# Retention's chunk loop: two output banks in turn, the outer product behind the next scores, and the state's masking, scaling and sum on GpSimd

## The reference, cut to what matters

```python
def _L3_attn_ref(x, Wq, Wk, Wv, gn_weight, gn_bias, Wout):   # 16 heads of 8
    Q = jnp.einsum('bld,hde->bhle', x, Wq)
    K = jnp.einsum('bld,hde->bhle', x, Wk)
    V = jnp.einsum('bld,hde->bhle', x, Wv)
    Dm = _decay_mask(Lq)                      # gamma_h ** (l - m) for m <= l, else 0
    scores = jnp.einsum('bhle,bhme->bhlm', Q, K) * Dm[None] / math.sqrt(HEAD_DIM)
    out = jnp.einsum('bhlm,bhme->bhle', scores, V)
    ...                                       # statistics over each head's whole length
    return combined @ Wout
```

## Time and profile before

| | us |
|---|---|
| median of 3 runs (2124.52 to 2133.64) | 2124.52 |
| the profiled execution: its own time | 2124.77 |
| the profiled execution: its span | 2123.0 |
| PE busy over the span | 1987.1 |
| DVE busy over the span | 1468.1 |
| ACT busy over the span | 1012.4 |
| POOL busy over the span | 260.6 |
| the chunk loop, first scores to last output (1923.67 to 1976.47) | 52.8 |

### The profile page before, as it was taken

How to read it: one execution, slowest core, us unless ns; L and a number is a source line. 1 busy time by engine, 2 the same in 40 slices (tenths; PEclk the granted TensorE clock), 3 DMA queues, 4 the chain that set the end, 5 groups by cost and what they waited for, 6 DMA issues and landing times.

```text
span 2123.0 us, 38784 instructions
## 1 busy us (share of the span) xinstructions
PE 1987.1 (94%) x13148; PEld 1242.4 (59%) x13148; DVE 1468.1 (69%) x4162; ACT 1012.4 (48%) x1898; POOL 260.6 (12%) x408
## 2 busy tenths in 40 slices
PE   7999999998999899999999998999997899998898
PEld 3523333333678556666666665778674677774576
DVE  6679999994566556666666666466658545877786
ACT  4347767776334355555555553345433333342233
POOL 2252212111027200000000000073000000000000
PEclk9989999999999999999999999999999999999999
DMA  6210000000027400000000000256100000000000
GB/s 238 32 63 26 26 23 28 23 23 24 16 74 220 123 1 1 1 0 0 0 0 0 0 1 1 75 164 206 51 1 0 1 1 1 1 1 2 1 1 21
DMA packets 62912, 78.07 MB, mean 37 GB/s; under 512 B 18954, under 2 KB 36638, under 8 KB 62017
## 3 DMA queue, kind: packets, MB, share of 16 engines
q1 hardware_dynamic: 57536, 67.18, 10.1%
q0 software_dynamic: 4672, 8.99, 1.7%
q10 hardware_dynamic: 576, 0.26, 0.1%
HBM read 64.14 MB, written 10.88 MB: 35 GB/s over the span
## 4 chain that ended last, share of the span: by engine, by line
PE 83%; DVE 7%; ACT 5%; issue 3%; DMA 1%; SPq 1%; ACTq 0%; POOL 0%; DVEq 0%; POOLq 0%
PE ps L455 13%; PE ps L434 12%; PE ps L1033 7%; PE ps L1067 6%; PE ps L2644 6%; PE ps L2607 6%; PE ps L2628 5%; PE ps L1050 4%; PE ps L835 3%; PE ps L846 3%; PE ps L2081 2%; PE ps L1017 2%; PE ps L1079 2%; ACT arena L1170 1%; PE ps L1039 1%
## 5 line engine op out<-in xcount | busy, mean ns | idle before, releaser
L455 PEld LDWEIGHTS ps<-l_w,arena 128*128 128x128 f32 x2560 | 335.4, 192 | 161.2 <-issue 144.1
L2894 DVE TENSOR_REDUCE arena<-ps 128x1 f32<-128x512 f32 x512 | 325.9, 684 | 40.9 <-PE ps L2607 40.9
L455 PE MATMUL ps<-l_w,arena 128*128 128x128 f32 x2560 | 339.3, 276 | 6.0 <-ACT arena L506 5.0
L434 PE MATMUL ps<-xnT,l_w 128*128 128x512 f32 x640 | 330.5, 599 | 3.0 <-ACT xnT L265 3.0
L2799 ACT ACTIVATE arena<-ps 128x1024 f32<-128x1024 f32 x256 | 252.6, 1022 | 102.1 <-PE ps L2628 101.4
L1233 DVE TENSOR_REDUCE arena<-ps 128x1 f32<-128x128 f32 (+7 forms) x256 | 178.6, 749 | 158.8 <-PE ps L1039 158.7
L588 DVE SCALAR_TENSOR_TENSOR x<-ps,comb,x 128x128 f32<-128x128 f32 x576 | 162.2, 344 | 151.6 <-PE ps L455 149.8
L506 ACT ACTIVATE arena<-ps,l_b 128x512 f32<-128x512 f32 x192 | 131.7, 687 | 216.2 <-PE ps L434 215.7
L1178 ACT ACTIVATE arena<-ps 128x512 f32<-128x512 f32 (+1 forms) x192 | 85.4, 489 | 231.5 <-PE ps L1050 231.4
L1170 ACT ACTIVATE arena<-ps,arena 128x128 f32<-128x128 f32 (+7 forms) x256 | 187.0, 745 | 13.2 <-DVE arena L1233 13.2
L2607 PE MATMUL ps<-arena 72*128 72x512 bf16 x512 | 184.3, 389 | 1.8 <-DVE arena L2894 1.1
(11 more groups left out here) (441 smaller groups left out, 2676.2 us busy)
## 6 DMA issues: line engine op xcount, KB each, us to landing
arena<-in_l_w SPq DMA_DIRECT2D x124, 256.0 KB
l_w<-in_l_w SPq DMA_DIRECT2D x2, 2048.0 KB, 14.4
l_w<-in_l_w SPq DMA_DIRECT2D x4, 1024.0 KB, 12.5
arena<-s_parts_q SPq DMA_DIRECT2D x28, 144.0 KB
arena<-s_parts_k SPq DMA_DIRECT2D x28, 144.0 KB
arena<-l_y_rows SPq DMA_DIRECT2D x12, 256.0 KB
s_parts_q<-arena SPq DMA_DIRECT2D x6, 256.0 KB, 3.4
s_parts_k<-arena SPq DMA_DIRECT2D x2, 768.0 KB, 5.3
```

What stands on the lines that cost most here:

```text
L434: pe.matmul(k.ps[:, n % 2, :], w.w1[:, e, f * P:(f + 1) * P], k.xnT[:, g * GW:(g + 1) * GW], start=True, stop=True).then_inc(s.hidden_mm.s ...
L455: ins = pe.matmul(k.ps[:, 2 + e % 4, j * P:(j + 1) * P], w.h[:, n % 2, j * P:(j + 1) * P], w.w2[:, e, f, :], start=(f == 0 and j == 0), st ...
L2894: dve.tensor_reduce(s.nm2[:, place, qt, half:half + 1], k.ps[:, bank, :], AX.X, ALU.max, negate=True)\
```

## The change

The output of chunk n goes to bank 6 + n % 2 instead of always bank 6. PE's order in turn n becomes: wait for the copy of chunk n - 2, cross term n, scores n + 1, wait for the copy of chunk n - 1, outer product n, output n. The outer product goes to the second 128 columns of the other bank (13 - bank), where chunk n - 1's output had been.

The state update leaves DVE. ACT copies the outer product from PSUM to `KV` in SBUF (a new `outer(n)`, between the copy of chunk n - 1's output and `spread(n + 1)`), and POOL does the rest: for a first chunk S = KV * block; for the others S = S * gC, KV = KV * block, a wait for both, and S = S + KV. POOL waits for ACT's copy before the first of them. Three semaphores of the projections are merged into one, `proj`, with counts to match; no order changes by it.

```diff
@@ -1495,9 +1495,9 @@
 
     def __init__(self, k, n, w):
         self.norm, self.w = Norm(k, n), w
-        self.q_mm = k.sem(f"{n}_q_mm")
-        self.k_mm = k.sem(f"{n}_k_mm")
-        self.kv_mm = k.sem(f"{n}_kv_mm")
+        self.proj = k.sem(f"{n}_proj")
+        self.outer_out = k.sem(f"{n}_outer_out")
+        self.masking = k.sem(f"{n}_masking")
         self.qd_out = k.sem(f"{n}_qd_out")
         self.k_out = k.sem(f"{n}_k_out")
         self.kv_out = k.sem(f"{n}_kv_out")
...
@@ -1530,6 +1530,21 @@
 def retention_pool(pool, k, s):
     pool.wait_ge(*s.free)
     pool.memset(s.vm[:, :, :], 0.0).then_inc(s.cleared, 1)
+    w, steps = s.w, 0
+    pool.wait_ge(w.loaded, w.loads)
+    for n in range(NT):
+        u = s.updates(n)
+        if n % s.CHUNKS == s.CHUNKS - 1:
+            continue
+        pool.wait_ge(s.outer_out, u + 1)
+        if n % s.CHUNKS == 0:
+            pool.tensor_tensor(s.S, s.KV, w.block[:, :], ALU.mult).then_inc(s.state, 1)
+            continue
+        pool.tensor_scalar(s.S, s.S, w.gC[:, 0:1], None, ALU.mult).then_inc(s.masking, 1)
+        pool.tensor_tensor(s.KV, s.KV, w.block[:, :], ALU.mult).then_inc(s.masking, 1)
+        steps += 2
+        pool.wait_ge(s.masking, steps)
+        pool.tensor_tensor(s.S, s.S, s.KV, ALU.add).then_inc(s.state, 1)
 
 
 def retention_tensor(pe, k, s):
...
@@ -1575,21 +1590,25 @@
     scores(0)
     for n in range(NT):
         c = n % s.CHUNKS
+        bank = 6 + n % 2
+        if n >= 2:
+            pe.wait_ge(s.o_out, n - 1)
+        if c:
+            pe.wait_ge(s.state, s.updates(n))
+            pe.matmul(k.ps[:, bank, 0:P], s.S, s.qd[:, n * P:(n + 1) * P], start=True, stop=False,
+                      skip_group_check=True)
+        if n + 1 < NT:
+            scores(n + 1)
         if n >= 1:
             pe.wait_ge(s.o_out, n)
-        if c:
-            pe.wait_ge(s.state, s.updates(n))
-            pe.matmul(k.ps[:, 6, 0:P], s.S, s.qd[:, n * P:(n + 1) * P], start=True, stop=False,
-                      skip_group_check=True)
         if c < s.CHUNKS - 1:
-            pe.matmul(k.ps[:, 7, 0:P], s.kd[:, n, :], s.v[:, n, :], start=True, stop=True).then_inc(s.outer, 1)
-        if n + 1 < NT:
-            scores(n + 1)
+            pe.matmul(k.ps[:, 13 - bank, P:2 * P], s.kd[:, n, :], s.v[:, n, :], start=True, stop=True,
+                      skip_group_check=True).then_inc(s.outer, 1)
         pe.wait_ge(s.vm_out, n + 1)
         pe.wait_ge(s.decayed, 2 * n + 2)
         for m in range(4):
             for q in range(4):
-                ins = pe.matmul(k.ps[32 * q:32 * q + 32, 6, 0:P],
+                ins = pe.matmul(k.ps[32 * q:32 * q + 32, bank, 0:P],
                                 s.vm[:, n % 2, P * m + 32 * q:P * m + 32 * q + 32], s.pT[n % 2][:, 4 * q + m, :],
                                 start=(c == 0 and m == 0), stop=(m == 3), tile_position=(0, 32 * q),
                                 skip_group_check=True)
...
@@ -1630,11 +1649,21 @@
         act.activation(dst.rearrange("p m (q z) -> p m q z", z=32)[:, :, :, 0:8],
                        s.v[:, n, :].rearrange("p (q m d) -> p m q d", m=4, d=8), ACT.Copy).then_inc(s.vm_out, 1)
 
+    def outer(n):
+        u = s.updates(n)
+        act.wait_ge(s.outer, u + 1)
+        if u:
+            act.wait_ge(s.state, u)
+        act.activation(s.KV, k.ps[:, 7 - n % 2, P:2 * P], ACT.Copy).then_inc(s.outer_out, 1)
+
     spread(0)
     spread(1)
+    outer(0)
     for n in range(NT):
         act.wait_ge(s.o_mm, 4 * (n + 1))
-        act.activation(s.oT[:, n * P:(n + 1) * P], k.ps[:, 6, 0:P], ACT.Copy).then_inc(s.o_out, 1)
+        act.activation(s.oT[:, n * P:(n + 1) * P], k.ps[:, 6 + n % 2, 0:P], ACT.Copy).then_inc(s.o_out, 1)
+        if n + 1 < NT and (n + 1) % s.CHUNKS < s.CHUNKS - 1:
+            outer(n + 1)
         if n + 2 < NT:
             spread(n + 2)
 
...
@@ -1681,15 +1710,6 @@
             dve.tensor_tensor(s.pT[n % 2][:, 8 * half:8 * half + 8, :],
                               k.ps[:, s.half(i), :].rearrange("p b (h l) -> p (b h) l", l=P),
                               every(w.mask, 8), ALU.mult).then_inc(s.decayed, 1)
-        if c < s.CHUNKS - 1:
-            dve.wait_ge(s.outer, s.updates(n) + 1)
-            if c == 0:
-                dve.tensor_tensor(s.S, k.ps[:, 7, 0:P], w.block[:, :], ALU.mult).then_inc(s.state, 1)
-                dve.wait_ge(s.state, s.updates(n) + 1)
-            else:
-                st.done(dve.tensor_tensor(s.KV, k.ps[:, 7, 0:P], w.block[:, :], ALU.mult))
-                dve.scalar_tensor_tensor(s.S, s.S, w.gC[:, 0:1], s.KV, ALU.mult, ALU.add).then_inc(s.state, 1)
-                dve.wait_ge(s.state, s.updates(n) + 1)
         if n >= GT and n % GT == 0:
             part_stats(n // GT - 1)
     st.done(part_stats(NG - 1))
```

More of the change, by code:

```diff
@@ L1547, in retention_tensor @@
             pe.wait_ge(s.qd_out, g - 1)
-        pe.matmul(k.ps[:, bank, :], w.wq[:, :], k.xnT[:, cols], start=True, stop=True).then_inc(s.q_mm, 1)
+        pe.matmul(k.ps[:, bank, :], w.wq[:, :], k.xnT[:, cols], start=True, stop=True).then_inc(s.proj, 1)
         if g >= 2:
             pe.wait_ge(s.k_out, g - 1)
-        pe.matmul(k.ps[:, bank + 1, :], w.wk[:, :], k.xnT[:, cols], start=True, stop=True).then_inc(s.k_mm, 1)
+        pe.matmul(k.ps[:, bank + 1, :], w.wk[:, :], k.xnT[:, cols], start=True, stop=True).then_inc(s.proj, 1)
         if g >= 2:
@@ L1558, in retention_tensor @@
                                 start=True, stop=True)
-            ins.then_inc(s.kv_mm, 1)
+            ins.then_inc(s.proj, 1)
     def scores(n):
@@ L1657, in retention_vector @@
             front_rows(dve, k, s.norm, NG - 1)
-        dve.wait_ge(s.q_mm, g + 1)
+        dve.wait_ge(s.proj, 4 * g + 1)
         dve.tensor_tensor(tiles(s.qd[:, cols]), tiles(k.ps[:, bank, :]), every(w.qdec, GT),
                           ALU.mult).then_inc(s.qd_out, 1)
-        dve.wait_ge(s.k_mm, g + 1)
+        dve.wait_ge(s.proj, 4 * g + 2)
         dve.tensor_tensor(tiles(s.kT[:, cols]), tiles(k.ps[:, bank + 1, :]), every(w.kinv, GT),
                           ALU.mult).then_inc(s.k_out, 1)
-        dve.wait_ge(s.kv_mm, 2 * g + 1)
+        dve.wait_ge(s.proj, 4 * g + 3)
         dve.tensor_tensor(s.kd[:, g * GT:(g + 1) * GT, :], tiles(k.ps[:, bank + 2, :]), every(w.kdec, GT),
                           ALU.mult).then_inc(s.kv_out, 1)
-        dve.wait_ge(s.kv_mm, 2 * g + 2)
+        dve.wait_ge(s.proj, 4 * g + 4)
         dve.tensor_copy(s.v[:, g * GT:(g + 1) * GT, :], tiles(k.ps[:, bank + 3, :])).then_inc(s.kv_out, 1)
```

## The result

The changed kernel took 2136.66 us as a median of 7 runs (2134.68 to 2142.02), the kernel before 2128.94 beside it (7 runs, 2124.52 to 2133.64). The ratio is 1.0043, with a 95% interval of 1.0026 to 1.006: slower by 0.3 to 0.6%, some 9 us. The medians themselves are 7.7 us apart. The prediction had 2130, +0.25%.

What follows compares the result with a forecast made beforehand. PE has work in all but 0.35 of a 3.27 us turn, the output's copy; DVE is nearly as full. Twelve turns of 3.87 add 7.2, other turns save 1.9: +5.3, about 2130 us; 8-in-10 range 2119 to 2139.

Steps and rivals of the forecast that it cites:

- the state's path: From the outer product over ACT and POOL to the next cross term: 2.09 us, cover 1.13, so PE waits 0.96.
- The size of a turn: Loop turns fed by three POOL instructions go from 3.27 to 3.87 us; over 12 turns +7.2.
- The forecast's upper bound: Slower POOL waits (0.51, not 0.08) give 2135.2; POOL's start and a late outer product end add 0.3 a turn: 2138.8.
- The other turns: Loop's start, turns 7 and 8 and the last output together save 1.9 us.
- Turn 7: Turn without an outer product: 2.69 us instead of 3.05, -0.36.
- Turn 8: Turn without a cross term: 2.42 us instead of 3.04, -0.62.
- Masks and POOL: In the loop, DVE's masks were taken not to contend with POOL's instructions: no cost.
- buys nothing of its own: DVE loses 0.63 us of work a turn, with no gain in time from that.
- C + 1.12: Masks of the next chunk start about 1.12 us after the turn's cross term starts.
- the rival of slow hand-offs: Waits between POOL's products and sum, and POOL's start after ACT, cost 0.43 more a turn or above: 2136.8; chance 0.21.
- PE's pace: Path after the outer product stays under 1.13; PE runs through at 2.91 us a turn: 2118.3; chance 0.09.
- Masks and clock in the loop: Two rivals: masks delay POOL, +1.2 us a turn, 2144, chance 0.07; PE's clock falls, +30 us, 2153, chance 0.03.

Runs made afterwards that it cites:

- decay_early: Changed kernel, but POOL scales the state as soon as the cross term has read it; turn 3.48, loop 54.1 us, one execution of 2124.77.
- outer_first: Changed kernel with the outer product again ahead of the next scores; turn 3.04, loop 49.7 us, ratio to the kernel before 0.9983.
- keep_clock: Changed kernel, outer product ahead of scores, state scaled early, 5 and 4 matmuls of nothing added in PE's waits behind the loop; ratio to before 0.998.
- pool_one_bank: Kernel before with only the state's move to ACT and POOL, one output bank and old order kept; turn 3.27, ratio 0.9995.

## Why the prediction was right, and where its numbers were off

- **What sets a turn**: right. The prediction's sum for the state's path has each piece in the chain of the changed kernel, in its order. The experiments bear it out: decay_early shortens the turn by what the path loses (0.59 of 0.60), and outer_first by about the cover that the path gains (1.03, the scores' 1.07). PE waits 1.1 a turn, 0.96 was said.
- **The size of a turn**: 3.87 was said, 4.07 measured; +9.6 over 12 turns instead of +7.2. The term that was mis-sized is the hand-offs. POOL to PE took 0.14, not the 0.05 taken from ACT to PE. The outer product's end as ACT sees it came 0.45 after the scores (0.43 + 0.02), not 0.36 (0.22 + 0.14): the 0.22 was its piece of the chain when the next matmuls followed it, not when someone waits for its end. Those two make 0.18 of the 0.20. The products and sum on POOL were priced well: 0.60, 0.43 and 0.46 against 0.60, 0.43 and 0.43. The forecast's upper bound had put the slack on POOL's own hand-offs (0.51), which stayed at 0.07.
- **Whose the 0.14 is**: not POOL's alone. ACT's copy reached PE in 0.04 nearly everywhere, but in 0.14 at the outer product of n = 8 in four traces, as in outer_first below. DVE's last mask reached the last output in 0.14 wherever that output waited for it. In the code each 0.14 stands where the wait that ended last is the second of two in a row on PE, and each 0.04 where it is the only one or the first. No run was made to separate this from other causes.

```profile
1944.95 0.29 ACT arena L1664
1945.24 0.14 issue
1945.37 0.46 PE ps L1603 x2
```

- **The other turns**: -1.9 was said, -1.6 came. The start gave -0.2, the last output -0.7 (1.59 after its cross term), as said. Turn 7 gave -0.5 instead of -0.36. Turn 8 gave only -0.16 instead of -0.62: its scores took 1.46, not 1.07, since behind a turn as short as 2.5 their second half waits for the first half-mask, and its outer product took 0.42, not 0.22; the output's 1.01 instead of 1.13 gave a little back.
- **Masks and POOL**: right. POOL's 128x128 products and sums took 454 to 462 ns on the mean in every kernel here, with masks running. The Trainium skill's rule (SBUF — State Buffer, "Who interferes with whom") that such a mask does not contend with GpSimd agrees with that. Its factor of two for GpSimd (GPSIMD Engine Reference, "Engine selection") is more than the 0.455 to 0.28, 1.6, of these rows, in which DVE's instruction reads one input from PSUM and POOL's reads both from SBUF.
- **DVE**: "buys nothing of its own" was right for the changed kernel. But that the masks start at C + 1.12 was wrong: a mask starts about 1.2 after the scores' start, not 0.6, because all four scores matmuls end nearly together: in the changed kernel's turn at 1943.92 the last records of the two halves end within 0.02 of each other, at 1945.04 to 1945.06. It cost the forecast nothing, since there was room.
- **After the loop**: not foreseen. The stretch behind it is 1.0 longer (8.85 against 7.81), at a lower granted clock. Loop and stretch together are +9.0, and the ratio gives 9.2 (0.0043 x 2128.94); but its interval reaches from 5.5 to 12.8 and the medians are 7.7 apart, so the runs can't tell +8.0 from +9.0. All other profiled kernels but keep_clock have 8.35 to 8.86 there, pool_one_bank (whose loop is as long as that of before) 8.86 too. Why the one trace of before has 7.81 stays open, and this 1.0 may not be the change's.
- **The range**: 2136.66 is inside 2119 to 2139, but outside the forecast's own 2127 to 2134, and it all but meets the 2136.8 of the rival of slow hand-offs, whose mechanism (0.51 instead of 0.08 between POOL's instructions) did not happen; that agreement is chance. A part of the distance is the base: the kernel before had 2124.52 as the median of 3 runs and 2128.94 as that of 7. From the second, +5.3 gives 2134.2.
- **The rivals**: the ratio came out 0.43% above before (the medians, 0.36%), inside 0.5%. PE's pace needs another order (outer_first) and is 3.04, not 2.91, for the copy's sake. POOL's own hand-offs were not slow (0.07 and 0.09). The late end of the outer product stood in the upper bound only, the longer way from POOL to PE in no bound. Masks and clock in the loop did not happen.

## What to carry to other kernels

When a serial step leaves the busy engine for an idle one, count the cover behind its start, not the idle engine's spare time: here the same POOL work was free with 2.1 us of cover and left PE idle for 1.1 us a turn with 1.0. A change that is two changes (a move and a reorder) may be good in one and bad in the other; the pair that lost here wins a little (3.1 us of the loop, a ratio of 0.9983) with one matmul moved back. And with two buffers, look at what else was put into them: the wait for the copy came back through the outer product that shares the bank.

## What the runs showed of the hardware

In the changed kernel POOL's completion reached PE in 0.14 us in every turn and ACT's reached POOL in 0.09; ACT's reached PE in 0.04, or in 0.14 in one turn of four kernels, so it does not go by the engine alone. A POOL instruction that waited for the one before it started 0.07 after it. With nine matmuls of nothing in two waits of 1.6 and 1.3 us, the one trace taken had a granted clock of 1.00 where three other traces had 0.61 to 0.78.
